# Taking TensorE's unread products out of the end of a graph layer

## The chip, the cores and the metric

The kernel runs on one core of a Trainium2 chip. The metric is the device time of one execution in microseconds (us). A profile of one execution goes with it; its rows are quoted by their line numbers in the kernel's source. Engines are written as the profile has them: PE is TensorE (PEld its weight loads), DVE is VectorE, ACT is ScalarE, POOL is GpSimd, SP is SyncE; a "q" behind a name (SPq, POOLq) is the engine's own queue, issuing DMAs or waiting.

## What is computed

A graph layer with 6250 nodes of 96 features and 100000 edges, sorted by their target node, with 4 features each. The reference, cut to what matters:

```python
h = jnp.maximum(_layernorm(x, axis=-1), 0.0)

def _mlp(h, W, b, gamma, beta):
    h = jax.nn.relu(h @ W + b)
    mu = jnp.mean(h, axis=0)
    var = jnp.mean(jnp.square(h - mu), axis=0)
    return gamma * (h - mu) * jax.lax.rsqrt(var + EPS) + beta

node_feat = _mlp(h, W_node, b_node, g_node, beta_node)
edge_feat = _mlp(edge_attr, W_edge, b_edge, g_edge, beta_edge)
message = jnp.concatenate([h[row], h[col], edge_feat], axis=1)
message = _mlp(message, W_msg, b_msg, g_msg, beta_msg)
agg = jax.ops.segment_sum(message, col, num_segments=N)
out = x + agg + node_feat
```

The messages are normalized over all edges, so their mean and variance are known only when the last edge has been worked on. The kernel therefore sums the messages before normalization and scales the sums at the end.

## The kernel before

The work has three stages. First, up to about 83 us, the nodes are normalized and a table of their products with the first third of the message weights, `p_table`, is made; the edge features are split into bf16 parts and written out as `x_stack`. Then, to about 280 us, a first pass over all edges takes the statistics of the edge features, the second table `q_table` is made and the node features are computed (PE lines 744 to 818). The third stage, from 280 us on, is the main loop over 196 groups of 512 edges (`NG` = 196; the last group has 160 edges, in two tiles of 128), unrolled and software-pipelined on each engine.

For one group, POOL gathers 512 rows of `p_table` into a ring of buffers (line 528, four indirect DMAs for a group); two late groups' rows (`FAR`) come by many small loads of ACT and SP instead. SP loads the group's columns of `x_stack` (line 487) and rows of `q_table` (line 496). PE makes the edge features and the one-hot selectors (lines 838 and 844), then the sums before the ReLU into `pc` (`products`, line 859). DVE adds the gathered rows (line 1126), ACT applies the ReLU into `hm` (line 694), and PE multiplies `hm` with itself and the selectors (`window_sum`, line 870): this gives the sums for a window of 96 nodes and a Gram matrix for the statistics. DVE adds both to `gram` and `agg` (lines 1132 and 1134; the profile names `agg` by its buffer, `big_a`). PE's order for a step is `edges` of two groups on, `products` of the next group, `window_sum` of this one.

Behind the loop, DVE and ACT make the message scale and shift from the Gram matrix in 13 small steps (lines 1183 to 1195), PE transposes the result (line 913), DVE copies it to `s_diag` (line 1198), and PE multiplies it with the window sums in 13 products, 12 of 512 nodes and one of 106 (`NQ` = 13, line 920). These are fp32; each shows as two matmul records in the profile, as does every fp32 product here. They go to four banks of PSUM in turn, DVE adds what is left to each (line 1203), and SP stores it (line 514).

The function `keep_clock(n)` issues n bf16 products of 128x128 by 128x512 into the bank `pa[:, 1, :]` (line 823). Nothing reads them and they carry no semaphore. They are issued at four places, all near the end of PE's program: 8 before the window sum of the last group but one, 4 before that of the last group (`W_GATHER`), 9 behind the last window sum, before PE waits for `fold_ready` (`W_SCALES`), and 2 behind the transpose, before PE waits for `diag_kept` (`W_DIAG`).

Of the kernel before, what the change touches and what calls it, by code (L numbers as in the profile page):

```python
# [21 lines left out]
GROUP = TPG * TILE  # L22
NG = -(-E // GROUP)
# [52 lines left out]
BACKLOG = 110  # L76
FAR_P1 = 9 * (P1_LOOPS - P1_PEELED - 1)
HW = WIN + C + 1


W_GATHER, W_SCALES, W_DIAG = (8, 4), 9, 2


def graph_layer(nc, x_rows, x_nodes, x_t, src_cols, dst_cols, dst_rows, row_bases, tile_bases, edge_rows, packed, w_edge,
# [8 lines left out]
    with ExitStack() as ctx:  # L93
        def sb(name, shape, dt=fp32):
            return ctx.enter_context(nc.sbuf_tensor(name, shape, dt))
# [19 lines left out]
        xs = sb("xs", [P, 4, 2 * GROUP], bf16)  # L115
# [24 lines left out]
        ident_b = sb("ident_b", [P, P], bf16)  # L140
# [19 lines left out]
        pa = ctx.enter_context(nc.psum_tensor("pa", [P, 2, 512], fp32))  # L160
# [106 lines left out]
        def at(i, j):  # L267

            return i + j // BODY, j % BODY

        def num(i, j):
            return i * BODY + j

        def exists(i, j):

            return not isinstance(i, int) or 0 <= num(i, j) < NG

        def wait(eng, s, value):

            if not isinstance(value, int) or value > 0:  # L280
                eng.wait_ge(s, value)

        def tiles(i, j):
            return LAST_TILES if isinstance(i, int) and num(i, j) == NG - 1 else TPG

        def passes(eng, body):

            body(0)
            with eng.Fori(1, LOOPS - 2) as i:
                body(i)  # L290
            body(LOOPS - 2)
            body(LOOPS - 1)
# [25 lines left out]
        def far_indices(engine, p):  # L318

            at_tile = FAR[0] * TPG  # L320
            _, at_node = nc.values_load_multi_w_load_instructions(  # L321
                src_idx[p:p + 1, at_tile:at_tile + FAR_T], [engine], min_val=0, max_val=N,
                skip_runtime_bounds_check_because="a node of an edge, below N by the kind of input")
            return at_node
# [72 lines left out]
        def _(sp):  # L397
# [18 lines left out]
            for s, name in enumerate(("hi", "mid", "lo")):  # L416
                sp.wait_ge(split_step, 2 * s + 1)
                for k, (part, _) in enumerate(STACK):
                    if part == name:
                        sp.dma_start(stack_rows(k), splits[:, s, :]).then_inc(stack_stored, 16)  # L420
# [60 lines left out]
            with sp.If(outside < 1):  # L481
                for g in range(NG):
                    i, j = at(0, g)
                    if g % 2 == 0:

                        wait(sp, hot_lin, g - 2)
                        sp.dma_start(xs[0:KX, j // 2, :], x_stack[:, g * GROUP:(g + 2) * GROUP]).then_inc(  # L487
                            x_main[j // 2], 16)
                        _, at_node = nc.values_load_multi_w_load_instructions(  # L489
                            bases[0:1, NG + g * TPG:NG + (g + 2) * TPG], [mybir.EngineType.SP], min_val=0,  # L490
                            max_val=N - 1,
                            skip_runtime_bounds_check_because="a node of an edge, below N by the kind of input")

                    wait(sp, pre_summed, g - 3)
                    for t in range(tiles(0, g)):
                        sp.dma_start(w3q[M1:M1 + TWIN, j, t, :],  # L496
                                     q_table[bass.ds(at_node[g % 2 * TPG + t], TWIN), :]).then_inc(q_in[j], 16)
                    for n in far_part(g, FAR_P1, (P - FAR_BY_ACT) * FAR_T, 0):
                        load_far(n)
                    if j == BODY - 1:  # L500
                        load_res(i)
# [230 lines left out]
        def _(pe):  # L732
# [84 lines left out]
            pe.wait_ge(shift_ready, 1)  # L817
            nc.tensor.matmul(pd[0:M1, 0, 0:C], t_col[:, :], w3[:, :], start=True, stop=True).then_inc(shift_made, 1)

            def keep_clock(n):  # L820

                for _ in range(n):
                    nc.tensor.matmul(pa[:, 1, :], ident_b[:, :], xs[:, 1, 0:GROUP], start=True, stop=True)

            pe.wait_ge(flag_ready, 1)
            outside = pe.value_load(flag[0:1, 0:1], min_val=0, max_val=2 * P)
            pe.wait_ge(main_ready, 1)
            with pe.If(outside < 1):
                def edges(i, j):

                    i, j = at(i, j)
                    if not exists(i, j):
                        return
                    g, n = num(i, j), tiles(i, j)
                    if j % 2 == 0:
                        pe.wait_ge(x_main[j // 2], i * 16 + 16)
                    wait(pe, edge_relu, g - 1)
                    nc.tensor.matmul(pa[:, j % 2, 0:n * TILE], we_stack[:, :],  # L838
                                     xs[:, j // 2, j % 2 * GROUP:j % 2 * GROUP + n * TILE],
                                     start=True, stop=True).then_inc(edge_lin, 1)  # L840
                    wait(pe, hot_built, g - 1)
                    for t in range(n):
                        at_edge = j % 2 * GROUP + t * TILE
                        last = nc.tensor.matmul(pb[:, j % 2, t * WIN:(t + 1) * WIN],  # L844
                                                xs[:, j // 2, at_edge:at_edge + TILE], hot_coef[:, :],
                                                start=True, stop=True)
                    last.then_inc(hot_lin, 1)

                def products(i, j):

                    i, j = at(i, j)
                    if not exists(i, j):
                        return
                    g, n = num(i, j), tiles(i, j)
                    pe.wait_ge(edge_relu, g + 1)
                    pe.wait_ge(q_in[j], i * (16 * TPG) + 16 * n)
                    wait(pe, msg_relu, g - 1)
                    for t in range(n):
                        last = nc.tensor.matmul(pc[:, j % 2, t * C:(t + 1) * C], r_sb[:, j % 2, t * TILE:(t + 1) * TILE],  # L859
                                                w3q[:, j, t, :], start=True, stop=True)  # L860
                    last.then_inc(pre_summed, 1)

                def window_sum(i, j):

                    g, n = num(i, j), tiles(i, j)
                    pe.wait_ge(msg_relu, g + 1)
                    wait(pe, win_added, g - 1)
                    pe.wait_ge(hot_built, g + 1)
                    for t in range(n):
                        last = nc.tensor.matmul(pd[0:M1, j % 2, 0:HW], hm[:, j, t, WIN:HW], hm[:, j, t, :],  # L870
                                                start=(t == 0), stop=(t == n - 1))
                    last.then_inc(win_summed, 1)

                edges(0, 0)
                edges(0, 1)
                products(0, 0)

                def fast(i):
                    for j in range(BODY):
                        edges(i, j + 2)  # L880
                        products(i, j + 1)
                        if isinstance(i, int) and num(i, j) >= NG - 2:

                            keep_clock(W_GATHER[num(i, j) - (NG - 2)])
                        window_sum(i, j)
                passes(pe, fast)
            with pe.Else():
                with pe.Fori(0, NG) as g:
# [3 lines left out]
                                     start=True, stop=True).then_inc(gen_lin, 1)  # L892
# [6 lines left out]
                    for t in range(TPG):  # L899
                        last = nc.tensor.matmul(pd[0:M1, 1, 0:M1], hm[:, 0, t, WIN:HW], hm[:, 0, t, WIN:HW],  # L900
                                                start=(t == 0), stop=(t == TPG - 1))
                    last.then_inc(gen_gram, 1)
                    with pe.Fori(0, GEN_WINS) as w:
                        pe.wait_ge(gen_hot, g * GEN_WINS + w + 1)
                        for t in range(TPG):
                            last = nc.tensor.matmul(pd[0:M1, 0, 0:WIN], hm[:, 0, t, WIN:HW], hm[:, 0, t, 0:WIN],
                                                    start=(t == 0), stop=(t == TPG - 1))
                        last.then_inc(gen_win, 1)

            keep_clock(W_SCALES)  # L910

            pe.wait_ge(fold_ready, 1)
            nc.tensor.transpose(pa[0:M1, 0, 0:C], fold[:, :], ident[0:C, 0:C]).then_inc(fold_turned, 1)
            keep_clock(W_DIAG)
            pe.wait_ge(diag_kept, 1)
            pe.wait_ge(messages_done, 1)
            for q in range(NQ):
# [3 lines left out]
                                 start=True, stop=True).then_inc(out_made, 1)  # L921
# [353 lines left out]
```

## Time and profile before

| | us |
|---|---|
| median of 3 runs | 996.18 (995.7 to 998.44) |
| the profiled execution's own time | 996.0 |
| its span, first to last instruction | 994.1 |
| PE busy | 759.2 (76%) |
| POOL busy | 732.0 (74%) |
| DVE busy | 531.6 (53%) |
| ACT busy | 369.7 (37%) |

The busy shares are means over stages with different limits, so they do not say what an edit in one stage is worth. The page also cuts the span into 40 slices of 24.9 us; a digit in a slice is the busy share in tenths, and PEclk is TensorE's granted clock in tenths of full speed. The chain of waits is followed back from the last instruction: each step is what released the next, or the instruction before it on its engine. The timeline lists instructions in order of time, merged where equal ones follow each other. The granted clock of a stretch is a mean over it: the clock has two levels, 2.4 GHz (1.00) and 1.2 GHz (0.50).

### The profile page before, as it was taken

The numbers are of one execution on the slowest core, as the hardware profiler recorded it, in microseconds if no ns is written. First come the engines' busy times: TensorE is split into PE (matmuls) and PEld (weight loads), VectorE is DVE, ScalarE is ACT, GpSimd is POOL, SyncE is SP. The second block draws the span as 40 slices with busy tenths as digits, with TensorE's granted clock in tenths as the row PEclk, the third lists the DMA queues.
The fourth block names the chain that finished last, engine by engine and source line by source line (L and its number), as shares of the span: only waits on it lengthen the run. The fifth ranks groups of instructions, "written<-read, shape, count | busy, mean of one in ns | idle before, by whom it ended". The sixth has DMA issues, their size and how long they took to land.

```text
span 994.1 us, 22967 instructions
## 1 busy us (share of the span) xinstructions
PE 759.2 (76%) x4820; PEld 605.1 (61%) x4820; DVE 531.6 (53%) x1422; ACT 369.7 (37%) x624; POOL 732.0 (74%) x778
## 2 busy tenths in 40 slices
PE   2735786676369999999999997777776776677687
PEld 2604562222158888888888886666665665566573
DVE  8577878878735555555555554343433333333345
ACT  3733696666323333333333332222222222222230
POOL 6777777777777777777777777777777777777770
PEclk9856797556569999999999999998999788887899
DMA  9575533333533333333333332332332322222223
GB/s 295 128 286 151 129 74 80 74 76 80 149 70 73 73 76 73 72 75 73 74 75 73 75 73 65 64 65 63 66 67 63 66 64 58 61 58 61 58 57 103
DMA packets 95826, 87.43 MB, mean 88 GB/s; under 512 B 67365, under 2 KB 71989, under 8 KB 95624
## 3 DMA queue, kind: packets, MB, share of 16 engines
q0 software_dynamic: 24768, 38.09, 17.8%
q1 hardware_dynamic: 68992, 47.18, 17.7%
q10 hardware_dynamic: 1992, 1.50, 0.6%
q14 instruction: 67, 0.55, 0.2%
q8 instruction: 7, 0.11, 0.0%
HBM read 68.80 MB, written 14.54 MB: 84 GB/s over the span
## 4 chain that ended last, share of the span: by engine, by line
SPq 39%; issue 19%; POOL 12%; PE 11%; DMA 10%; ACT 4%; DVE 4%; ACTq 1%; DVEq 0%; POOLq 0%
SPq L496 20%; POOL ring L528 12%; SPq L446 6%; SPq L489 5%; DMA ring<-p_table,src_idx 4%; DMA xs<-x_stack 4%; PE pc L750 3%; SPq L432 2%; SPq L321 2%; SPq L487 2%; PE pd L870 2%; DMA big_a<-zeros 2%; PE pc L859 1%; SPq L473 1%; ACT r_sb L646 1%
## 5 line engine op out<-in xcount | busy, mean ns | idle before, releaser
L528 POOL DMA_INDIRECT ring<-p_table,src_idx x726 | 686.2, 945 | 221.4 <-issue 202.8
L870 PE MATMUL pd<-hm 128*97 128x193 f32 x1564 | 316.9, 348 | 18.2 <-ACT hm L694 18.2
L870 PEld LDWEIGHTS pd<-hm 128*97 128x97 f32 x1564 | 258.8, 176 | 28.6 <-ACT hm L694 20.9
L859 PE MATMUL pc<-w3q,r_sb 128*128 128x96 f32 x1564 | 223.6, 288 | 37.9 <-ACT r_sb L684 36.1
L684 ACT ACTIVATE r_sb<-pa 128x512 f32<-128x512 f32 x196 | 116.8, 596 | 307.0 <-issue 133.5
L859 PEld LDWEIGHTS pc<-w3q,r_sb 128*128 128x128 f32 x1564 | 197.6, 198 | 43.9 <-issue 24.7
L1126 DVE TENSOR_TENSOR pc<-pc,ring 128x384 f32<-128x384 f32 x194 | 109.5, 564 | 157.3 <-POOLq L557 94.3
L1110 DVE TENSOR_SCALAR hm<-pb 128x384 f32<-128x384 f32 x196 | 109.1, 557 | 134.2 <-PE pb L844 85.8
L694 ACT ACTIVATE hm<-pc 128x384 f32<-128x384 f32 x196 | 96.2, 491 | 189.8 <-DVE pc L1126 182.0
L1047 DVE BATCH_NORM_STATS2 edge_st<-r_sb 96x512 f32 (+1 forms) x196 | 121.6, 675 | 35.8 <-ACT r_sb L646 34.4
L838 PE MATMUL pa<-xs,we_stack 128*128 128x512 bf16 x196 | 79.4, 405 | 64.6 <-DMA xs<-x_stack 64.0
L1132 DVE TENSOR_TENSOR gram<-gram,pd 97x97 f32<-97x97 f32 x196 | 50.0, 255 | 90.0 <-PE pd L870 86.0
L792 PE MATMUL pa<-xs,we_stack 128*97 128x512 bf16 x98 | 44.9, 554 | 52.5 <-DMA xs<-x_stack 44.8
L844 PEld LDWEIGHTS pb<-hot_coef,xs 128*128 128x128 bf16 x782 | 57.8, 102 | 36.2 <-issue 8.1
L838 PEld LDWEIGHTS pa<-xs,we_stack 128*128 128x128 bf16 x196 | 19.8, 101 | 87.1 <-issue 63.1
L844 PE MATMUL pb<-hot_coef,xs 128*128 128x96 bf16 x782 | 68.5, 213 | 0.0
L646 ACT ACTIVATE r_sb<-pa 96x1024 f32<-96x1024 f32 x49 | 49.9, 1019 | 41.3 <-PE pa L792 28.4
L792 PEld LDWEIGHTS pa<-xs,we_stack 128*97 128x97 bf16 x98 | 11.7, 163 | 79.2 <-ACT r_sb L646 50.5
L528 POOL DMA_INDIRECT ring<-in_x_rows,src_idx x48 | 45.5, 949 | 18.1 <-issue 14.0
L646 ACT ACTIVATE r_sb<-pb 96x1024 f32<-96x1024 f32 x49 | 49.9, 1019 | 4.9 <-DVE edge_st L1047 4.0
L1134 DVE TENSOR_TENSOR big_a<-big_a,pd 97x96 f32 x196 | 48.6, 248 | 0.0
L750 PE MATMUL pc<-pk,big_a 128*128 128x96 f32 x200 | 34.1, 327 | 14.9 <-ACT ring L657 8.3
(116 smaller groups left out, 419.2 us busy)
## 6 DMA issues: line engine op xcount, KB each, us to landing
w3q<-q_table SPq DMA_DIRECT2D x782, 11.2 KB
ring<-p_table,src_idx POOLq DMA_INDIRECT x726
ln_buf<-p_table ACTq DMA_DIRECT2D x704, 0.4 KB
xs<-x_stack SPq DMA_DIRECT2D x98, 72.0 KB
x_stack<-ring SPq DMA_DIRECT2D x6, 980.0 KB, 5.6
xs<-x_stack SPq DMA_DIRECT2D x98, 60.0 KB, 1.9
ln_buf<-p_table SPq DMA_DIRECT2D x320, 0.4 KB
ring<-in_x_nodes SPq DMA_DIRECT2D x5, 480.0 KB, 9.2
```

What stands on the lines that cost most here:

```text
L496: sp.dma_start(w3q[M1:M1 + TWIN, j, t, :], q_table[bass.ds(at_node[g % 2 * TPG + t], TWIN), :]).then_inc(q_in[j], 16)
L528: nc.gpsimd.indirect_dma_start(out=ring[:, tile * C:(tile + 1) * C], out_offset=None, in_=table, in_offset=bass.IndirectOffsetOnAxis(ap=id ...
L646: nc.scalar.activation(r_sb[0:C, k % 2, :], (pa, pb)[k % 2][0:C, :, :].rearrange("c a b -> c (a b)"), ACT.Relu).then_inc(p1_relu, 1)
L684: nc.scalar.activation(r_sb[:, j % 2, 0:n], pa[:, j % 2, 0:n], ACT.Relu).then_inc(edge_relu, 1)
L694: nc.scalar.activation(hm[:, j, 0:n, WIN:WIN + C], pc[:, j % 2, 0:n * C].rearrange("p (t c) -> p t c", c=C), ACT.Relu).then_inc(msg_relu, 1)
L838: nc.tensor.matmul(pa[:, j % 2, 0:n * TILE], we_stack[:, :], xs[:, j // 2, j % 2 * GROUP:j % 2 * GROUP + n * TILE], start=True, stop=True) ...
L844: last = nc.tensor.matmul(pb[:, j % 2, t * WIN:(t + 1) * WIN], xs[:, j // 2, at_edge:at_edge + TILE], hot_coef[:, :], start=True, stop=True)
L859: last = nc.tensor.matmul(pc[:, j % 2, t * C:(t + 1) * C], r_sb[:, j % 2, t * TILE:(t + 1) * TILE], w3q[:, j, t, :], start=True, stop=True)
L870: last = nc.tensor.matmul(pd[0:M1, j % 2, 0:HW], hm[:, j, t, WIN:HW], hm[:, j, t, :], start=(t == 0), stop=(t == n - 1))
L1047: last = V.bn_stats(edge_st[:, bass.ds(u * 2 + half, 1), :].rearrange("c a s -> c (a s)"), r_sb[0:C, k % 2, half * GROUP:half * GROUP + n])
L1110: V.tensor_scalar(hm[:, j, 0:n, 0:WIN], pb[:, j % 2, 0:n * WIN].rearrange("p (t w) -> p t w", w=WIN), 0.0, None, ALU.max).then_inc(hot_bui ...
L1126: V.tensor_tensor(pc[:, j % 2, 0:n], pc[:, j % 2, 0:n], rows, ALU.add).then_inc(pre_added, 1)
```

## The change

The constants, the function `keep_clock` and its three calls (for four places) are taken out. Nothing else is changed.

```diff
-W_GATHER, W_SCALES, W_DIAG = (8, 4), 9, 2
...
-            def keep_clock(n):
-
-                for _ in range(n):
-                    nc.tensor.matmul(pa[:, 1, :], ident_b[:, :], xs[:, 1, 0:GROUP], start=True, stop=True)
-
...
                         edges(i, j + 2)
                         products(i, j + 1)
-                        if isinstance(i, int) and num(i, j) >= NG - 2:
-
-                            keep_clock(W_GATHER[num(i, j) - (NG - 2)])
                         window_sum(i, j)
...
-            keep_clock(W_SCALES)
-
             pe.wait_ge(fold_ready, 1)
             nc.tensor.transpose(pa[0:M1, 0, 0:C], fold[:, :], ident[0:C, 0:C]).then_inc(fold_turned, 1)
-            keep_clock(W_DIAG)
             pe.wait_ge(diag_kept, 1)
```

## Rows read from the trace of the kernel before

**Rows 1.** The head of the page: the span, and PE and its clock in 40 slices.

```profile
span 994.1 us, 22967 instructions
...
PE   2735786676369999999999997777776776677687
...
PEclk9856797556569999999999999998999788887899
```

**Rows 2.** The chain of waits over the end: start us, us, what.

```profile
970.72 3.19 DMA ring<-p_table,src_idx
...
974.90 0.91 PE pd L870 x4
...
979.15 0.32 PE pa L913
979.48 0.43 PE pa L823 x2
979.91 1.87 PE pc L920 x4
981.78 1.72 PE pb L920 x4
...
990.40 0.75 DVE big_b L1203
```

**Rows 3.** Timeline, 969 to 992: start us, us, engine, line, operation, tiles, shapes [idle before].

```profile
969.23 1.89 PE L823 MATMUL pa<-xs,ident_b 128*128 128x512 bf16 x8
...
972.08 1.55 PE L870 MATMUL pd<-hm 128*97 128x193 f32 x8 [0.96 <-ACT hm L694]
...
973.47 1.02 PE L823 MATMUL pa<-xs,ident_b 128*128 128x512 bf16 x4
...
974.90 0.90 PE L870 MATMUL pd<-hm 128*97 128x193 f32 x4 [0.40 <-ACT hm L694]
...
975.64 2.10 PE L823 MATMUL pa<-xs,ident_b 128*128 128x512 bf16 x9
...
979.31 0.60 PE L823 MATMUL pa<-xs,ident_b 128*128 128x512 bf16 x2
979.51 0.26 DVE L1198 COPY s_diag<-pa 97x96 f32<-97x96 f32 x1 [0.42 <-PE pa L913]
...
981.81 10.16 SPq L514 DMA_DIRECT2D out_t<-big_b  x13
...
984.40 1.60 DVE L1203 SCALAR_TENSOR_TENSOR big_b<-pc,sc,big_b 96x512 f32<-96x512 f32 x2
```

**Rows 4.** One stretch: length, PE, PEld, DVE, ACT, POOL busy; clock, DMA share, GB/s.

```profile
966.00:990.00 24.00, 21.23 (x87) 11.16 (x86) 13.62 (x37) 1.79 (x5) 4.45 (x5) 1.00 0.30 85
```

**Rows 5.** Timeline of PE in the main loop, its first product after long idle stretches.

```profile
658.52 0.40 PE L838 MATMUL pa<-xs,we_stack 128*128 128x512 bf16 x1 [3.30 <-DMA xs<-x_stack]
...
682.94 0.60 PE L838 MATMUL pa<-xs,we_stack 128*128 128x512 bf16 x1 [3.77 <-DMA xs<-x_stack]
...
730.47 0.60 PE L838 MATMUL pa<-xs,we_stack 128*128 128x512 bf16 x1 [3.16 <-DMA xs<-x_stack]
...
714.47 0.39 PE L838 MATMUL pa<-xs,we_stack 128*128 128x512 bf16 x1 [2.99 <-DMA xs<-x_stack]
```

**Rows 6.** Stretches behind such idle time in the main loop, columns as in rows 4.

```profile
658.50:662.50 4.00, 3.98 (x20) 3.73 (x21) 1.12 (x2) 1.09 (x2) 3.09 (x4) 0.57 0.30 62
...
683.00:690.00 7.00, 7.00 (x34) 6.03 (x35) 2.10 (x5) 1.13 (x3) 5.47 (x6) 0.54 0.32 67
...
730.50:734.50 4.00, 4.00 (x20) 3.65 (x21) 1.12 (x2) 1.03 (x2) 3.09 (x4) 0.58 0.27 55
...
952.00:956.00 4.00, 3.76 (x16) 3.06 (x17) 0.68 (x2) 0.68 (x2) 3.09 (x4) 0.57 0.21 44
...
714.50:718.50 4.00, 4.00 (x35) 3.69 (x36) 1.71 (x5) 1.09 (x2) 3.08 (x4) 1.00 0.30 60
```

**Rows 7.** Timeline of PE: eight window-sum records at either level of the clock.

```profile
952.24 2.86 PE L870 MATMUL pd<-hm 128*97 128x193 f32 x8 [1.96 <-ACT hm L694]
...
957.08 1.55 PE L870 MATMUL pd<-hm 128*97 128x193 f32 x8 [0.29 <-ACT hm L694]
```

## The prediction

> **What bounds the kernel now.** I read four views in this order: the head of the page, the chain of waits over the end, the timeline of the same end, and the granted clock by stretches. All times below are those of the profiled execution: its span is 994.1 us [rows 1] and its own time 996.0 us, so 1.9 us lie outside the span. The median of the three runs is 996.18 us (995.7 to 998.44), 0.2 us above that. I make the sum against 996.0. About 0.3%, or 3.0 us, is what a measurement of this kernel can tell from no change.
>
> The change touches only what TensorE (PE) does after the last gathers, so the end is where to look. The chain [rows 2] says who is late there, in order: up to 973.9 us it is GpSimd's gather of the last rows (a DMA of 3.19 us), then the last window sum on PE (0.91 us from 974.90), then a string of small VectorE steps up to the transpose of 0.32 us at 979.15, then the output products of line 920. These stand in the chain without a break from 979.91 to 990.40 us: 1.87 us for the first four records (two products), 1.72 us for each later four. After them comes one VectorE add of 0.75 us. So PE is the bound of the last 10.5 us, at 0.86 us a product. VectorE's add takes 1.60 us for two products, 0.80 each, and SyncE (SP) issues 13 stores in 10.16 us, 0.78 each [rows 3]. Both are faster than PE by only 0.06 to 0.08 us a product.
>
> The granted clock is 1.00 (2.4 GHz) from 966 to 990 us [rows 4]. Thus all products run at the upper level now.
>
> **What the change removes: 23 products of line 823.** They stand at four places in the timeline [rows 3]:
> - Eight from 969.23 us (1.89 us) and four from 973.47 us (1.02 us). The window sums behind them start at 972.08 and 974.90; the first eight are over by 971.12 and the four by 974.49. So PE waits anyway, and the gather of [rows 2] hides both groups. Taking them out gains nothing.
> - Nine from 975.64 us (2.10 us), over by 977.74. The transpose waits for VectorE until 979.15. Hidden as well: nothing gained.
> - Two from 979.31 us. The chain puts 0.43 us on them [rows 2], but the copy that the first product needs runs from 979.51 for 0.26 us [rows 3], to 979.77. Only what lies between its end and 979.91 can be won, 0 to 0.14 us with the handover in it. I take a gain of 0.05 us.
>
> No wait, semaphore, DMA or other engine's instruction is changed; no queue is passed by anything. The removed records write a bank of PSUM that nobody reads and wait for nothing.
>
> **What the change exposes: the clock.** Without the 23 records PE would be idle from about 969.3, where the first of them starts, to 972.08 (2.8 us), busy for 1.55, idle for 1.3, busy for 0.9, idle from 975.8 to the transpose at about 979.2 (3.4 us), idle again behind it until 979.8, and then dense [rows 2, 3]. The trace does not show that ending, so I bound its cost by the nearest rows, the places in the main loop where a gather or a load was late.
>
> [Rows 5] are PE's returns from long idle stretches in that loop. Of those over 3.0 us there are four; three stand there, with 3.30, 3.77 and 3.16 us, and behind each of them the clock was at the lower level (1.2 GHz) when work was taken up again, or fell to it at once: the mean granted clock of these stretches is 0.57, 0.54 and 0.58 [rows 6]. Behind the fourth row, an idle stretch of 2.99 us, it stayed at 1.00, while one of 1.96 us ahead of 952.24 [rows 7] was followed by 0.57. The 3.4 us ahead of the transpose belong to those that brought the fall. So I take it that the products start at, or soon fall to, 1.2 GHz.
>
> How long does it stay low? In a stretch of length L with mean clock c the low time is 2 x (1 - c) x L. [Rows 6]: 4.0 us at 0.57 give 3.4 us, 4.0 at 0.58 give 3.4, 4.0 at 0.57 (from 952) give 3.4, and 7.0 us at 0.54 give 6.4. In all of them PE was busy nearly throughout. So the bounds are 3.4 and 6.4 us, the short one in three of four rows, and the mean is 4.2; the end has more than one idle stretch ahead of the dense work, so I take 4.5 us.
>
> What does a low microsecond cost? The same eight records of the window sum took 2.86 us in a low stretch and 1.55 us in a high one [rows 7], a factor of 1.85. In T us of low clock PE does T / 1.85 of high-clock work, so it loses 0.46 T: 1.6 us for 3.4, 2.1 us for 4.5, 2.9 us for 6.4. Nothing gives it back: when the clock has returned, PE needs 0.86 us a product again and VectorE 0.80 behind it, so PE stays the bound and the loss reaches the end whole.
>
> A price from the Trainium skill (TensorE: Matmul & The Clock Gate, section "Back-to-back issue gap") stands beside that: it gives 512 columns 512/1.2 ns at the lower and 512/2.4 + 2.5 ns at the upper level, a factor of 1.98. By it a low microsecond would lose 0.49, and my 4.5 us would cost 2.2 and not 2.1 us; the row of this kernel, with its weight loads in it, decides, and no row shows the wide product itself at 1.2 GHz.
>
> Two small terms lie ahead of the products. If the clock falls already behind the first idle stretch of 2.8 us, the last two window sums are slow: the first (1.55 to 2.86 us from 972.08) ends at 974.94, about when the second starts, and the second's 0.90 us becomes 1.66, so +0.8 us on the chain. Of the two rows of 2 to 3 us one brought the fall and one did not, so I take half, 0.4 us (bounds 0 and 0.8). The transpose's 0.32 us [rows 2] becomes at most 0.27 us longer by the same factor; I take 0.1 us (bounds 0 and 0.3).
>
> Sum: 2.1 + 0.4 + 0.1 - 0.05 = +2.55 us, so 996.0 + 2.6 = 998.6 us, +0.26%. Lowest of the bounds with a fall: 1.6 + 0 + 0 - 0.14 = +1.5, 997.5. Highest: 2.9 + 0.8 + 0.3 - 0 = +4.0, 1000.0.
>
> **The rivals.**
> - The slow end, slower by over 0.3%: the fall comes in the first idle, both window sums and the transpose are slow, and the products begin so that the clock returns only after the long low stretch. Price +4.0 us, 1000.0 us; it decides from a low time of about 5.5 us on (0.46 x 5.5 + 0.5 = 3.0). For it speaks the stretch at 683 us (6.4 us low though PE was busy 7.00 of 7.00); against it that three of four rows are short.
> - The clock holds, not slower: the change then does nothing but take out hidden records, and the products keep 0.86 us each. The window sums and the transpose would have to be work enough. Price -0.14 to 0, so 995.9 us. For it speaks the idle stretch of 2.99 us that brought no fall; against it the 3.4 us ahead of the transpose, beside rows of 3.16 us and more that all did, and that so little work stands between the end's idle stretches.
> - The clock falls and does not come back: 10.5 us of products [rows 2] cost 0.85 x 10.5 = 8.9 us more, with the small terms some +9.5, 1005.5 us. The slices of the page [rows 1] show a long low part in the eighth to tenth digits of PEclk (5 5 6), so it can stay low; but PE there is 6 to 7 tenths busy, and the products leave no gap. The same page of the Trainium skill, section "Seeing it yourself", tells of a clock seen stuck low for a long time, which would be this case; no row shows it under unbroken work.
>
> **How the numbers follow.** The forecast (fall, return within the products, +1.5 to +3.0) gets 0.61, the slow end 0.25, the clock that holds 0.10, the clock that stays low 0.02, and 0.02 is left for a faster run by something I don't see. The runs of before spread by 2.7 us, and where in the ending the clock turns may differ from run to run, so the range goes from 996.7 to 1000.3 us: it holds the forecast, the slow end and the bounds, and leaves out the two small cases and the clock that holds. Slower by over 0.3% (above 999.0): the slow end and the stuck clock, 0.27. Within 0.3%: forecast and holding clock, 0.71. Faster: 0.02.
>
> **What would show it.** In the profile after: a granted clock under 1.00 somewhere between 972 and 987 us; the first fours of line 920 in the chain near 3.2 us and the later ones back at 1.72; a low time of 3.4 to 6.4 us; VectorE waiting for PE in the low part; all before 972 us unchanged. If the last window sum takes 1.6 us, the fall came early. I am wrong if the clock stays at 1.00 through the products, if the low products take clearly more or less than 1.85 times as long, or if VectorE or the stores turn out to hide the loss.

## The result, and the profile after

| | before | after |
|---|---|---|
| median, us (9 runs each) | 996.37 (995.7 to 998.44) | 999.09 (997.78 to 1000.22) |
| profiled execution, own time | 996.0 | 999.56 |
| its span | 994.1 | 997.4 |

The ratio is 1.0027, 95% interval [1.0018, 1.0036]: +2.7 us, between 1.8 and 3.6. The forecast was +2.6 us, to 998.6, in a range from 996.7 to 1000.3.

First the chain of waits over the end of the kernel after (start us, us, what). Its lines have moved up: the window sum is line 862 (870 before), the transpose 900 (913), the output products 906 (920), VectorE's last add 1189 (1203).

```profile
972.07 3.19 DMA ring<-p_table,src_idx
...
976.25 0.91 PE pd L862 x4
...
980.50 0.49 PE pa L900
...
981.33 3.73 PE pc L906 x4
985.06 1.86 PE pb L906 x4
986.92 1.72 PE pc L906 x4
...
993.82 0.75 DVE big_b L1189
```

Against [rows 2]: the first four records of the products take 3.73 us for 1.87, the second four still 1.86 for 1.72, and from the third four on they take 1.72 as before. The transpose takes 0.49 for 0.32. The last window sum has its 0.91 us unchanged. From the first product to VectorE's last add the chain has 993.82 - 981.33 = 12.49 us, 990.40 - 979.91 = 10.49 before: +2.00 us.

The granted clock of the same end, by stretches (columns as in [rows 4]):

```profile
968.00:978.00 10.00, 5.20 (x34) 4.38 (x32) 3.00 (x13) 1.47 (x4) 3.80 (x5) 1.00 0.12 25
978.40:981.30 2.90, 0.48 (x1) 0.24 (x1) 1.80 (x12) 0.20 (x1) 0.00 (x0) 0.50 0.00 0
981.30:985.20 3.90, 3.87 (x5) 1.53 (x6) 0.85 (x2) 0.00 (x0) 0.00 (x0) 0.50 0.03 9
985.20:994.00 8.80, 8.76 (x22) 3.26 (x20) 7.54 (x11) 0.00 (x0) 0.00 (x0) 1.00 0.67 206
```

Where [rows 4] had 1.00 throughout, the clock here is at 0.50 from 978.4, in PE's idle stretch ahead of the transpose, and the products run 3.9 us at that level. Then it returns and stays. Nothing hides the loss. VectorE's waits for the products in bank `pc` (engine, line, waited for: us in total, times, longest) show it standing behind PE. In the kernel before:

```profile
DVE big_b L1203 <- PE pc L920: 1.3, 1, 1.3
```

In the kernel after:

```profile
DVE big_b L1189 <- PE pc L906: 3.1, 2, 2.2
```

One thing in the profile was not foreseen: the last gather begins at 972.07 us, 1.35 us later than before ([rows 2], 970.72). The lag is there long before anything that the change touches: it is 0.39 us at the first gather of `p_table` (64.76 us, 64.37 before) and 0.85 us at the 501st of the 774 gathers (630.17, 629.32). So of the 3.3 us between the two spans 1.35 lie upstream of the end. To keep the two apart I read every kernel below by its **end**, the time from the start of the last gather to the end of the span: before 994.1 - 970.72 = 23.4 us, after 997.4 - 972.07 = 25.3 us.

### The profile page after: what moved, and what is told of

It reads as the page before. It is cut to its first block, busy times and chain, and to the rows that moved or that the text cites. A ratio compares the mean times of both kernels' runs of the same rounds, so it can differ in the third digit from the quotient of the medians.

```text
span 997.4 us, 22921 instructions
## 1 busy us (share of the span) xinstructions
PE 752.3 (75%) x4797; PEld 603.4 (60%) x4797; DVE 530.8 (53%) x1422; ACT 370.0 (37%) x624; POOL 733.2 (74%) x778
## 4 chain that ended last, share of the span: by engine, by line
SPq 31%; issue 20%; POOL 18%; DMA 12%; PE 10%; DVE 4%; ACT 4%; ACTq 1%; DVEq 0%; POOLq 0%
POOL ring L525 18%; SPq L493 15%; DMA ring<-p_table,src_idx 6%; SPq L443 4%; SPq L486 4%; DMA xs<-x_stack 3%; PE pc L747 2%; SPq L429 2%; SPq L484 2%; PE pd L862 2%; DMA big_a<-zeros 2%; SPq L318 2%; DVE edge_st L1033 1%; PE pc L851 1%; ACT r_sb L643 1%
## 5 line engine op out<-in xcount | busy, mean ns | idle before, releaser
L851 PEld LDWEIGHTS pc<-w3q,r_sb 128*128 128x128 f32 x1564 | 199.7, 200 | 47.1 <-issue 28.6
L789 PE MATMUL pa<-xs,we_stack 128*97 128x512 bf16 x98 | 41.7, 517 | 56.8 <-DMA xs<-x_stack 46.7
```

## The experiments

The theory is that of the prediction: without the unread products' work the clock falls ahead of the output products, and these pay. The rivals: that the number of records or the code's place counts and not the work; that one group of the 23 does everything; that the gathers became slower. "Kept" names the unread products that stay, by their number at each place. Each time is compared with that of the kernel before, measured beside it on the same chip.

| kernel | median us | before us | ratio, 95% interval | last gather starts | end, us |
|---|---|---|---|---|---|
| before | | | | 970.72 | 23.4 |
| after | 999.09 | 996.37 | 1.0027 [1.0018, 1.0036] | 972.07 | 25.3 |
| after, second profile | 999.65 (1 run) | 997.29 | | 970.75 | 27.1 |
| after, third profile | 999.92 (1 run) | 997.29 | | 971.91 | 26.0 |
| 9 and 2 kept | 996.43 | 995.95 | 1.0002 [0.9993, 1.0011] | 971.16 | 23.3 |
| 8 and 4 kept | 998.79 | 995.95 | 1.0026 [1.0015, 1.0036] | 970.32 | 26.3 |
| all 23, 8 columns wide | 999.05 | 995.95 | 1.0031 [1.0019, 1.0043] | 971.39 | 25.3 |
| 13 ahead of the transpose | 995.89 | 995.95 | 0.9998 [0.9989, 1.0007] | 970.76 | 23.4 |
| only the 9 kept | 998.20 | 997.29 | 1.0007 [0.9998, 1.0016] | 971.03 | 24.4 |
| only the 2 kept | 1000.11 | 997.29 | 1.0029 [1.0018, 1.0040] | 970.93 | 25.8 |

### One half of the change at a time

```diff
-W_GATHER, W_SCALES, W_DIAG = (8, 4), 9, 2
+W_GATHER, W_SCALES, W_DIAG = (0, 0), 9, 2
```

> Keeps the 9 and the 2 unread products behind the last window sum, takes out only the 8 and the 4 ahead of the last two window sums. I read the end as the time from the start of the last gather to the end of the span: 23.4 us in the kernel before (970.72 to 994.1), 25.3 us in the kernel after (972.07 to 997.4), so 1.95 us longer. Clock theory: the products of line 920 run mostly at 2.4 GHz since the 9 products stand right ahead of them; what is left of the loss is a slow last window sum at the most. End 23.4 to 24.4 us, time +0.0 to +0.8 us, about +0.4. Rival, that the number of records or the code's place costs the time: 12 of 23 records are gone, so about half of the loss, end 24.4 us with the products at 1.72 us a four, time +1.4 us. Rival, that it is the gather ahead of the end that became slower: end 23.4 us and the time still +1 us or more.

```diff
-W_GATHER, W_SCALES, W_DIAG = (8, 4), 9, 2
+W_GATHER, W_SCALES, W_DIAG = (8, 4), 0, 0
```

> Keeps the 8 and the 4 unread products, takes out the 9 and the 2 behind the last window sum. Clock theory: PE is idle for 3.3 us ahead of the transpose, so the transpose and the first products run at 1.2 GHz, both window sums at 2.4 GHz (0.90 us for the last four records). End 24.8 to 26.2 us, time +1.3 to +2.9 us, about +2.1, that is nearly the whole loss. Rival of the number of records: 11 of 23 gone, about half of the loss, end 24.4 us, +1.3 us. Together with the kernel that keeps the other half: if the clock is the cause, this one has most of the loss and the other little; if the number counts, both have half.

With the 9 and the 2 kept, the time can't be told from that of before (1.0002, the interval from -0.7 to +1.1 us). The chain of that kernel has the products at full speed:

```profile
979.60 0.32 PE pa L913
979.92 0.43 PE pa L823 x2
980.36 1.87 PE pc L920 x4
982.23 1.72 PE pb L920 x4
```

And its clock stays up, as the stretch from 966 to 990 us shows:

```profile
966.00:990.00 24.00, 20.32 (x92) 11.96 (x90) 14.17 (x40) 2.50 (x6) 4.72 (x5) 1.00 0.29 80
```

With the 8 and the 4 kept and the others out, the whole loss is there (1.0026). Its chain:

```profile
978.76 0.49 PE pa L913
...
979.59 3.73 PE pc L920 x4
983.32 2.91 PE pb L920 x4
986.23 1.72 PE pc L920 x4
```

Two stretches of it, through the window sums and from the first product on:

```profile
966.00:975.00 9.00, 7.65 (x47) 5.63 (x46) 2.62 (x11) 1.59 (x4) 4.04 (x5) 1.00 0.16 30
979.60:985.60 6.00, 6.00 (x7) 2.08 (x8) 2.03 (x3) 0.00 (x0) 0.00 (x0) 0.50 0.21 62
```

Most of the first eight records run low here, for 6.0 us, and the end of 26.3 us is a little over what I expected. So it is not the number of records, which would have given half to each: what stands behind the last window sum decides. Which of the two places there it is, this pair does not tell; the kernel with only the 2, below, does. This kernel also refutes the slower gathers as the cause: its last gather starts at 970.32, earlier than in the kernel before, and it still loses 2.6 us.

### The same records with little work in them

```diff
-                    nc.tensor.matmul(pa[:, 1, :], ident_b[:, :], xs[:, 1, 0:GROUP], start=True, stop=True)
+                    nc.tensor.matmul(pa[:, 1, 0:8], ident_b[:, :], xs[:, 1, 0:8], start=True, stop=True)
```

> All 23 unread products stay at their places, but with 8 columns for 512, so that their number, their weight loads and the code are those of the kernel before and only their work is gone. Clock theory: as the kernel after, the first four records of line 920 take 3 to 3.8 us for 1.87, end 25 to 26.5 us, time +1.9 to +3.5 us, about +2.6. Rival, that the number of instructions or the code's layout matters: as before, end 23.4 us, time +0. If weight loads alone keep the clock up: end 23.4 us with the clock at 1.00.

Program, number of records and weight loads are those of the kernel before; the time is that of the kernel after (1.0031). Its timeline:

```profile
976.33 0.37 PE L823 MATMUL pa<-xs,ident_b 128*128 128x8 bf16 x9
979.85 0.48 PE L913 MATMUL pa<-pk,fold 96*97 96x96 f32 x1 [3.15 <-DVE fold L1195]
...
980.67 3.73 PE L920 MATMUL pc<-big_a,s_diag 97*96 97x512 f32 x4 [0.32 <-DVE s_diag L1198]
```

The stretch from its first product on:

```profile
980.70:984.40 3.70, 3.70 (x5) 1.41 (x6) 0.75 (x1) 0.00 (x0) 0.00 (x0) 0.50 0.00 0
```

The nine take 0.37 us for 2.10 in [rows 3], and the clock falls as if they were not there. The layout of the code, the number of instructions and the weight loads are out as causes.

### Which group holds the clock

```diff
-W_GATHER, W_SCALES, W_DIAG = (8, 4), 9, 2
+W_GATHER, W_SCALES, W_DIAG = (0, 0), 9, 0
```

> Only the 9 unread products behind the last window sum stay; the 8, the 4 and the 2 are out. Clock theory: they fill the wait for the scales from about 975.6 to 977.7 us, but PE is idle before them, and behind them until the transpose and again until the first product, so the clock holds in some runs and falls late in others: end 23.3 to 25.1 us, time 0 to +1.7 us, about +0.7. Rival, that the 2 behind the transpose are what holds the clock: as the kernel with both of the end's groups out, +2 to +3 us and end 25 to 26.3 us.

```diff
-W_GATHER, W_SCALES, W_DIAG = (8, 4), 9, 2
+W_GATHER, W_SCALES, W_DIAG = (0, 0), 0, 2
```

> Only the 2 unread products behind the transpose stay. Clock theory: the idle stretch of 3.3 us ahead of the transpose is untouched, so the products start at 1.2 GHz; the first product waits for up to 0.3 us of slow unread products as well. End 24.7 to 26.6 us, time +1.3 to +3.2 us, about +2.3. Rival, that these 2 are enough: +0 and end 23.4 us.

With the 9 alone the time lies between the two kernels, +0.7 us, but its interval (-0.2 to +1.6 us) takes in no change, so whether the nine alone are enough stays open. In its profile the products run high, but the window sums do not. The chain:

```profile
973.77 3.55 PE pd L870 x12
...
980.67 0.34 PE pa L913
...
981.35 1.96 PE pc L920 x4
983.30 1.72 PE pb L920 x4
```

The stretches of the window sums with the nine, and of what follows:

```profile
974.40:978.00 3.60, 3.60 (x13) 2.64 (x12) 1.18 (x5) 0.33 (x1) 0.00 (x0) 0.53 0.00 0
978.00:990.00 12.00, 10.58 (x29) 4.02 (x28) 8.86 (x22) 0.20 (x1) 0.00 (x0) 1.00 0.38 113
```

The clock fell at about 974.4 us, behind an idle stretch, and the window sums and the nine worked it up again before the transpose. A gather landed late in that run as well (3.90 us from 968.53), so that all twelve window-sum records stand in one row from 973.77. It did not make the end longer by itself: at the upper level eight took 1.55 us ([rows 3]) and the four right behind them 0.70 (the chain of the kernel with 13, below), so by an estimate the twelve would have ended at 976.0, 5.0 us behind the start of the last gather, where the kernel before has 5.1 (975.81 - 970.72). They ended at 977.33, and the products behind them took no longer than before. So the 1.0 us by which this end is longer belongs to the slow window sums.

With the 2 alone the loss is whole (1.0029), so it is the idle stretch ahead of the transpose that has to be filled. At the lower level the two are in the way as well: 0.85 us for 0.43, and in the chain the products' piece begins 1.33 us behind the transpose's start (0.83 in the kernel after). Its chain:

```profile
979.39 0.48 PE pa L913
979.87 0.85 PE pa L823 x2
980.72 3.41 PE pc L920 x4
984.14 1.92 PE pb L920 x4
```

### The two moved ahead of the transpose

```diff
-W_GATHER, W_SCALES, W_DIAG = (8, 4), 9, 2
+W_GATHER, W_SCALES, W_DIAG = (8, 4), 13, 0
```

> The 2 unread products behind the transpose are moved ahead of it (13 and 0 for 9 and 2), the 8 and the 4 stay. They then end at about 978.6 us, ahead of the transpose at 979.15. It measures the term of -0.05 us (bounds -0.14 and 0) that I gave the 2. Clock theory: the clock stays at 1.00, the first product starts as soon as the copy is there, end 23.3 to 23.4 us, time -0.1 to 0. Rival, that the 2 are needed to hold the clock through the wait for the copy: the first products slow, end 25 us, +1.5 us.

The edit does a little more than the text above says: 13 are two more than 9 and 2, so 25 unread products are issued and not 23. The chain of that kernel:

```profile
974.53 0.86 PE pa L823 x4
975.39 0.70 PE pd L870 x4
...
979.43 0.34 PE pa L913
...
980.10 1.96 PE pc L920 x4
982.06 1.72 PE pb L920 x4
...
990.68 0.75 DVE big_b L1203
```

Its clock over the same stretch as in [rows 4]:

```profile
966.00:990.00 24.00, 22.92 (x100) 12.96 (x100) 13.96 (x39) 2.33 (x6) 4.48 (x5) 1.00 0.29 82
```

The clock holds without the two. What they cost behind the transpose is read from the timeline, since the chain lets a piece begin only where the one before it ends. The first products in the kernel before:

```profile
979.83 1.96 PE L920 MATMUL pc<-big_a,s_diag 97*96 97x512 f32 x4
```

In this kernel:

```profile
980.10 1.96 PE L920 MATMUL pc<-big_a,s_diag 97*96 97x512 f32 x4 [0.35 <-DVE s_diag L1198]
```

The first product starts 979.83 - 979.15 = 0.68 us behind the transpose with the two, and 980.10 - 979.43 = 0.67 us without them. From the transpose to VectorE's last add it is 11.25 us in both. So at the upper level the two cost nothing, and the time agrees (0.9998).

What I had not expected is the first row of the chain. The window sum of the last group but one started 972.98 - 972.08 = 0.9 us later than in [rows 3], and the four unread products behind it stand on the chain, ahead of the last window sum. They cost next to nothing even so: from the start of the last rows' add on VectorE to the end of that window sum it is 1.76 us (974.33 to 976.09), before 1.75 (974.06 to 975.81). But no slack was left: a little later, and they would have delayed it.

### The kernel after, twice more

> The kernel after once more, for a second profile of its end. In the first one the end (start of the last gather to the end of the span) was 25.33 us for 23.38 before, while the last gather itself began 1.35 us later than before (972.07 for 970.72). Theory: the longer end belongs to the change and the later gather to the run, so the end is 24.8 to 27.0 us again, and the last gather begins anywhere from 970.3 to 972.1. Rival, that the change also slows the gathers: the last gather begins at 972 again.

> The kernel after a third time, for a third profile of its end; as in the second look: end 24.8 to 27.0 us, last gather from 970.3 to 972.1 if its start belongs to the run. If the clock falls already ahead of the last window sums, their last four records take about 1.6 us for 0.90 and the end comes out at 26.5 us or more; in three profiles of endings without work ahead of the transpose the four took 0.90 us.

The second profile's chain:

```profile
970.75 3.26 DMA ring<-p_table,src_idx
...
975.00 1.62 PE pd L862 x4
...
979.95 0.49 PE pa L900
...
980.78 3.73 PE pc L906 x4
984.51 2.94 PE pb L906 x4
987.44 1.72 PE pc L906 x4
...
994.35 0.75 DVE big_b L1189
```

The stretches of the second profile through the last window sums and from the first product on:

```profile
973.00:977.00 4.00, 2.56 (x8) 1.37 (x6) 1.04 (x5) 0.33 (x1) 0.00 (x0) 0.52 0.02 3
980.70:986.80 6.10, 6.02 (x7) 2.09 (x8) 2.07 (x4) 0.00 (x0) 0.00 (x0) 0.50 0.21 61
```

The third profile's chain:

```profile
981.18 3.73 PE pc L906 x4
...
994.44 0.75 DVE big_b L1189
```

Its low stretch:

```profile
981.20:986.60 5.40, 5.40 (x7) 1.98 (x8) 1.49 (x2) 0.00 (x0) 0.00 (x0) 0.50 0.13 39
```

The end is longer in all three executions of the same kernel, by 1.9, 3.7 and 2.6 us; their mean is 2.8 us, near the measured +2.7. The longest, 27.1 us, lies just above what I expected. The last gather started at 972.07, 970.75 and 971.91 us, and in the other kernels between 970.32 and 971.39. With 970.75 the second profile starts it where the kernel before does, though the change is in it. Two of the three starts are the latest of all ten profiles, so the three starts alone do not clear the change. But the lag of the first profile is there from 64 us on, as said above, and that of the third stood at 0.64 us by the 501st gather (629.96 for 629.32): both grew far ahead of anything that the change touches. Where in the ending the clock falls also differs between executions: at about 973 us in the second profile, ahead of the last window sum, at 978.4 in the first and at about 979.8 in the third. In the first and the third the whole low stretch is 6.8 us long (978.4 to 985.2, 979.8 to 986.6). The first had 2.9 us of it over when its products began, the third 1.4.

## Why the prediction was right, step by step

- **The bound and its cover.** Right: PE's products are the chain's last stretch in every profile, and the loss came through to the end. The margins were misread. An add takes VectorE 0.75 us ([rows 2]) and a store's issue 0.32 us; the rows of 1.60 us for two adds and 10.16 us for 13 stores take in waits. Both engines had more room than I said, 0.11 and 0.54 us a product.
- **21 of the 23 are hidden.** Right in the kernel before; taking out the 8 and the 4 gave 1.0002. The kernel with 13 ahead of the transpose shows the limit: with the window sums late, four of them stood on the chain, just without a cost.
- **The two behind the transpose.** Taken as a gain of 0.05 us in bounds of 0 and 0.14. It is nothing: the first product starts 0.68 us behind the transpose with them and 0.67 without.
- **The clock falls.** Right, in all three profiles of the kernel after and in the three that left nothing wide between the last window sum and the transpose (8 and 4 kept, narrow, only the 2). The fourth idle stretch over 3.0 us in the main loop, which [rows 5] do not show, bears it out too: 3.80 us ahead of 849.57, and a clock of 0.62 from 849.5 to 854.
- **How long it stays low.** Mis-sized. I took 4.5 us of low products, above the mean of the main loop's rows; the three profiles have 3.9, 6.1 and 5.4, a mean of 5.1. The bounds of 3.4 and 6.4 held, but in part by luck. They came from rows in which PE was busy nearly throughout the low time; here the low stretches, 6.8 us long in the first and third profile and 13.6 in the second, began ahead of the products, and what counted was how much of one fell on them.
- **What a low microsecond costs.** Too low. The window sum's factor of 1.85 [rows 7] gave 0.46. The products' own is 3.41 / 1.72 = 1.98 for four in a row (only the 2 kept, against any later four), so 0.50; the first four came out at 3.73 us and not near the 3.2 that I named as a sign. The Trainium skill's price (TensorE: Matmul & The Clock Gate, "Back-to-back issue gap", 1.98 by its formulas) was the better one, and the rows now show it. From the first product's start to VectorE's last add, by the timeline, the three profiles have +1.9, +3.0 and +2.7 us for my +2.1.
- **The window sums.** I took half of 0.8 us, from two rows, of which one (1.96 us) was not in the range that I named. The main loop has nine idle stretches of 2 to 3 us, and in five of them the clock fell within 2 us after, so half was not far off for the loop. At the end they were slow in one of three profiles, 1.62 us for 0.91, so +0.7 there and 0.2 in the mean. That this term was too large and the two above too small is luck.
- **The transpose.** 0.49 for 0.32, +0.17, against 0.1 taken; from its start to the first product it is 0.83 us for 0.68, +0.15.
- **The rivals.** The slow end, priced at +4.0 us with a chance of 0.25, is the second profile: both its parts are there, slow window sums and 6.1 us of low products, and its end is 3.7 us longer. A clock that holds and one that stays low were seen in no profile of the kernel after. The mechanism of the forecast is shown; that the sum came out at +2.6 for a measured +2.7 is partly luck, as its terms erred to both sides. The end of a single execution is from 1.9 to 3.7 us longer.
- **What was to be unchanged.** I wrote that all before 972 us would be; the gathers came 1.35 us later in the first profile. The change is not the cause: the lag is there from the first gathers of `p_table` on, and the second profile doesn't have it at the end.

## What to carry to other kernels

Products that nobody reads can be worth their place where an engine waits and is the bound right after: here 5.6 us of PE time that waits anyway save 2.7 us, most of it slow products. What they had to fill was the idle stretch straight ahead of the dense work, and with real work; the twelve further up made no difference that could be measured. Put them where the engine waits for certain: with the clock low the two behind the transpose delayed the first product, with it high they cost and gave nothing, and with the window sums late four had no slack left.

## What the runs showed of the hardware

- 23 products with 8 columns, each with its weight load, did not keep the clock up where 23 with 512 columns at the same places did; the first four records that followed took 3.73 us in the one and 1.87 in the other.
- An fp32 product of 512 columns takes 1.98 times as long at the lower level, 0.85 us a record for 0.43 (3.41 for 1.72 in four); the window sum with 193 columns and its weight load took 1.78 (1.62 for 0.91) to 1.85 times as long (2.86 for 1.55).
- The same kernel's end differed by 1.8 us between executions (25.3 to 27.1) and the start of the last of its 774 gathers by 1.3 us (970.75 to 972.07). One pair of profiles would have put the latter down to the change.
